# First input ahead of the settings, the feed-forward of the last batch but one behind the last scores, the last gelu from PSUM, and projections in the scores' ring of PSUM banks

## What is computed

```python
q = layer_norm(transpose(x + pos))      # b, 512, 256
kv = layer_norm(transpose(ctx + pos))
Q, K, V = split(q @ Wq), split(kv @ Wk), split(kv @ Wv)     # 16 heads of 16
y = softmax(Q @ K.T / 4) @ V @ Wo
r = y + q
h = layer_norm(r)
out = gelu(h @ W1 + b1) @ W2 + b2 + r   # W1 256x512, W2 512x256
return transpose(out)
```

## Time and profile before

| | |
|---|---|
| median of 3 runs | 3221.22 us |
| lowest, highest | 3213.65, 3223.86 us |
| the profiled execution | 3225.38 us |
| its span in the trace | 3223.6 us |
| mean granted TensorE clock | 0.939 |
| PE busy | 2833.4 us (88%) |
| DVE busy | 1797.5 us (56%) |
| ACT busy | 1350.6 us (42%) |
| POOL busy | 881.5 us (27%) |

### The profile page before, as it was taken

The page is one execution under the profiler, slowest core; times in us unless marked ns, Lnnn a source line. Parts: engine busy times, 40 slices in busy tenths (PEclk is TensorE's granted clock), DMA queues, the critical chain, the costliest instruction groups (busy, mean ns, idle before and its releaser), DMA issues. The chain is left out here.

```text
span 3223.6 us, 41533 instructions
## 1 busy us (share of the span) xinstructions
PE 2833.4 (88%) x14752; PEld 1332.4 (41%) x14752; DVE 1797.5 (56%) x4426; ACT 1350.6 (42%) x2376; POOL 881.5 (27%) x722
## 2 busy tenths in 40 slices
PE   4999999888999999989999999987868888888895
PEld 1222222234555555546556555643322333333332
DVE  3777777724344433312565565656777577667641
ACT  0566666652333333332434333422324444555462
POOL 1577777763344443310010001011111010100000
PEclk7999999998999999899999999998978999999997
DMA  4444444320002000112333323234233232323300
GB/s 101 94 106 101 108 102 103 96 88 26 27 28 84 28 28 22 69 51 72 68 65 63 65 65 75 50 70 91 73 90 86 58 85 51 87 65 68 75 26 21
DMA packets 182335, 219.94 MB, mean 68 GB/s; under 512 B 40840, under 2 KB 135664, under 8 KB 175984
## 3 DMA queue, kind: packets, MB, share of 16 engines
q1 hardware_dynamic: 170064, 189.74, 25.6%
q0 software_dynamic: 6016, 20.98, 1.9%
q10 hardware_dynamic: 6048, 6.56, 0.6%
HBM read 146.90 MB, written 51.64 MB: 62 GB/s over the span
## 5 line engine op out<-in xcount | busy, mean ns | idle before, releaser
L1485 DVE TENSOR_REDUCE l_M<-PS 128x1 f32<-128x512 f32 x512 | 334.5, 682 | 148.1 <-PE PS L963 145.2
L1264 DVE TENSOR_REDUCE l_M<-PS 128x1 f32<-128x512 f32 x512 | 332.0, 684 | 149.0 <-PE PS L704 148.1
L1203 ACT ACTIVATE l_P<-PS 128x512 f32<-128x512 f32 x512 | 286.7, 598 | 258.2 <-PE PS L973 240.5
L1568 POOL TENSOR_TENSOR l_S<-l_P 128x512 f32<-128x512 f32 x256 | 328.0, 1313 | 88.7 <-ACT l_P L1046 88.7
L1046 ACT ACTIVATE l_P<-PS 128x512 f32<-128x512 f32 x512 | 281.4, 598 | 111.4 <-PE PS L713 109.8
L963 PE MATMUL PS<-l_KS,l_QS 97*128 97x512 bf16 x512 | 206.3, 413 | 105.2 <-DVE l_M L1485 73.7
L1323 DVE TENSOR_REDUCE l1a_M<-PS 128x1 f32<-128x512 f32 x256 | 158.8, 682 | 246.4 <-PE PS L768 246.4
L1391 DVE CUSTOM_DVE_ANT_0 l_JK<-PS,l_MK 128x256 f32<-128x256 f32 x512 | 195.7, 419 | 136.2 <-PE PS L881 133.2
L704 PE MATMUL PS<-l_KS,l_QS 97*128 97x512 bf16 x512 | 204.2, 414 | 45.3 <-DVE l_M L1264 20.1
L846 PE MATMUL PS<-l_w_mlp_w,l_H 128*128 128x512 f32 x512 | 233.4, 602 | 5.9 <-ACT l1a_P L1099 5.0
L594 PE MATMUL PS<-l_YT,l_w_mlp_w 128*128 128x256 f32 x1024 | 233.3, 384 | 2.9 <-ACT l_YT L1124 2.6
(11 more groups left out here) (248 smaller groups left out, 4746.1 us busy)
## 6 DMA issues: line engine op xcount, KB each, us to landing
l_QS<-q_scratch SPq DMA_DIRECT2D x128, 128.0 KB, 5.7
q_scratch<-l_T SPq DMA_DIRECT2D x96, 128.0 KB
l_QS<-q_scratch SPq DMA_DIRECT2D x32, 384.0 KB, 4.9
k_scratch<-l_T SPq DMA_DIRECT2D x96, 128.0 KB
l_KS<-k_scratch SPq DMA_DIRECT2D x32, 384.0 KB
l_QS<-q_scratch SPq DMA_DIRECT2D x32, 256.0 KB, 5.5
l_KS<-k_scratch SPq DMA_DIRECT2D x32, 256.0 KB
l_RB<-l_recs SPq DMA_DIRECT2D x32, 256.0 KB
```

Source lines behind the costliest of these rows:

```text
L1203: e.activation(t.P[quad % 4][:, m, :], PS[:, COUNTS.bank[st], :], ACT.Exp, scale=0.25).then_inc(q.sem("act.exp", st), 1)
L1264: e.tensor_reduce(t.M[i % 2][:, qt, hd:hd + 1], PS[:, COUNTS.bank[st], :], AX.X, ALU.max).then_inc(q.sem("dve.smax", st), 1)
L1485: e.tensor_reduce(t.M[i % 2][:, qt, hd:hd + 1], PS[:, COUNTS.bank[st], :], AX.X, ALU.max).then_inc(q.sem("dve.smax", st), 1)
L1568: x = e.tensor_tensor(t.S[j % 2][:, m, :], t.P[2 * j % 4][:, m, :], t.P[(2 * j + 1) % 4][:, m, :], ALU.add)
```

## The change

It has five parts.

1. `0.start` on SP no longer holds the six `ones_rows`: they are a step of their own, `0.start1`, behind the first `0.load`. The first item's `stack` 0 moves from 0.36 to 0.52, behind the writes of both scratches.
2. In ring: `0.proj`, `0.turn`, `3.proj` and `3.turn` fill banks of ring C in place of ring A.
3. For batch 6 (the last but one) `f4` moves from 5.6 (and 0.08 each) to 6.36 (and 0.02 each), `f5` from 6.05 and 6.15 to 6.5 and 6.55: behind the last `sc` and `vals` of batch 7, ahead of the last `f1`.
4. For batch 7 the separate `gelu` is dropped: `f4` on ScalarE applies Gelu with the bias straight from PSUM to SBUF, and each product of `f5` waits for the quarter of `l_G` that it reads.
5. Each batch is stored in two halves, one behind each `f5`.

```diff
-        return [..., (0.36, k("stack", 0)), ...
+        return [..., (0.36 if (b, h) > (0, 0) else 0.52, k("stack", 0)), ...
-    return order + [(-9, ("0.start", 0, 0, 0)), ...]
+    return order + [(-9, ("0.start", 0, 0, 0)), (0.69, ("0.start1", 0, 0, 0)), ...]
-            out += [...] + [(5.6 + 0.08 * n, k("f4", n)) for n in range(4)]
-            out += [(6.05, k("f5", 0)), (6.15, k("f5", 1))]
+            out += [...] + [((6.36 + 0.02 * n) if b == B - 2 else (5.6 + 0.08 * n), k("f4", n)) for n in range(4)]
+            out += [(6.5, k("f5", 0)), (6.55, k("f5", 1))] if b == B - 2 else [(6.05, k("f5", 0)), (6.15, k("f5", 1))]
-        elif (kind, j) == ("3.f4", 3):
+        elif (kind, j) == ("3.f4", 3) and b < B - 1:
             cut = [(kind, b, h, j), ("3.gelu", b, h, 0)]
-FILLS = {"0.proj": ("A", "dve.rest"), ..., "0.turn": ("A", "act.turn"),
+FILLS = {"0.proj": ("C", "dve.rest"), ..., "0.turn": ("C", "act.turn"),
-         ... "3.proj": ("A", "dve.rest"), ... "3.turn": ("A", "act.turn"),
+         ... "3.proj": ("C", "dve.rest"), ... "3.turn": ("C", "act.turn"),
 (tensor3)
             elif kind == "3.f5":
                 q.wait_ge("w23", ("3.start2", 0, 0, 0))
-                q.wait_ge("act.gelu", step("3.gelu", i))
-                bank = q.bank_empty(st)
-                products(q, PS[:, bank, :], [(t.w2[:, o, j * 128:j * 128 + 128], t.G[:, o, :])
-                                             for o in range(4)]).then_inc(q.sem("pe.f5", st), 1)
+                if b < B - 1:
+                    q.wait_ge("act.gelu", step("3.gelu", i))
+                bank = q.bank_empty(st)
+                for o in range(4):
+                    if b == B - 1:
+                        q.wait_ge("act.f4", step("3.f4", i, o))
+                    x = e.matmul(PS[:, bank, :], t.w2[:, o, j * 128:j * 128 + 128], t.G[:, o, :], start=(o == 0), stop=(o == 3), ...)
+                x.then_inc(q.sem("pe.f5", st), 1)
 (scalar3)
-                e.activation(t.G[:, j, :], PS[:, COUNTS.bank[st], :], ACT.Identity, bias=col["b13"][:, j:j + 1]
-                             ).then_inc(q.sem("act.f4", st), 1)
+                e.activation(t.G[:, j, :], PS[:, COUNTS.bank[st], :], ACT.Gelu if b == B - 1 else ACT.Identity,
+                             bias=col["b13"][:, j:j + 1]).then_inc(q.sem("act.f4", st), 1)
 (sync0)
                 row(q, t.bv, "bv0")
-                q.wait_ge("pool.start", st)
+            elif kind == "0.start1":
+                q.wait_ge("pool.start", ("0.start", 0, 0, 0))
                 ones_rows(q, t.Q + t.K, 512)
 (sync3)
-            elif kind == "3.f5" and j == 1:
+            elif kind == "3.f5":
                 q.wait_ge("dve.f5", st)
-                e.dma_start(tokens(out[b]), t.RT[:, :, :]).then_inc(q.sem("store", st), 16)
+                e.dma_start(tokens(out[b])[:, j, :], t.RT[:, j, :]).then_inc(q.sem("store", st), 16)
```

More of the change, by code:

```diff
@@ L25, in a1 @@
         k = lambda n, j=0: ("0." + n, b, h, j)
-        return [(0.1125, k("proj", 0)), (0.1625, k("split", 0)), (0.3625, k("proj", 1)), (0.4125, k("split", 1)), (0.36, k("stack", 0)), (0.6, k("stack", 1)), (0.61, k("mrow")),
+        return [(0.1125, k("proj", 0)), (0.1625, k("split", 0)), (0.3625, k("proj", 1)), (0.4125, k("split", 1)), (0.36 if (b, h) > (0, 0) else 0.52, k("stack", 0)), (0.6, k("stack", 1)), (0.61, k("mrow")),
                 (0.6125, k("v", 0)), (0.8625, k("v", 1))]
@@ L52, in layer0_order @@
     order = [(2 * b + h + beat + at, st) for b, h in ITEMS for beat, part in enumerate((a0, a1, a2, c, p)) for at, st in part(b, h)]
-    return order + [(-9, ("0.start", 0, 0, 0)), (17.4, ("mark", 3, 0, 0)), (19.4, ("mark", 4, 0, 0))]
+    return order + [(-9, ("0.start", 0, 0, 0)), (0.69, ("0.start1", 0, 0, 0)), (17.4, ("mark", 3, 0, 0)), (19.4, ("mark", 4, 0, 0))]
 BEGIN1 = 18.35
@@ L149, in steps @@
             out += [(5.22 + 0.02 * n, k("onewton", n)) for n in range(3)] + [(5.3 + 0.03 * n, k("f2b", n)) for n in range(4)]
-            out += [(5.45, k("f3", 0)), (5.51, k("f3", 1))] + [(5.6 + 0.08 * n, k("f4", n)) for n in range(4)]
-            out += [(6.05, k("f5", 0)), (6.15, k("f5", 1))]
+            out += [(5.45, k("f3", 0)), (5.51, k("f3", 1))] + [((6.36 + 0.02 * n) if b == B - 2 else (5.6 + 0.08 * n), k("f4", n)) for n in range(4)]
+            out += [(6.5, k("f5", 0)), (6.55, k("f5", 1))] if b == B - 2 else [(6.05, k("f5", 0)), (6.15, k("f5", 1))]
         return out
@@ L273 @@
     "3.out1": [("put", 4, 1), ("me1", 1, 4)], "3.fetch": [("fetch", 2, 1)], "3.inv": [("rec", 2, 1)],
[1 row of a table removed]
[1 row of a table added]
 }
 JOINS = {("0.mrow", "ks"), ("0.sout1", "put"), ("1.sums1", "put"), ("2.out1", "put"), ("3.out1", "put")}
-FILLS = {"0.proj": ("A", "dve.rest"), "0.v": ("A", "dve.v"), "0.smax": ("A", "dve.smax"), "0.turn": ("A", "act.turn"),
+FILLS = {"0.proj": ("C", "dve.rest"), "0.v": ("A", "dve.v"), "0.smax": ("A", "dve.smax"), "0.turn": ("C", "act.turn"),
          "0.sc": ("C", "act.exp"),
@@ L699, in tensor0 @@
                 qt, hd = divmod(j, 8)
-                q.wait_ge("set", ("0.start", 0, 0, 0))
+                q.wait_ge("set", ("0.start1", 0, 0, 0))
                 q.wait_ge("qs", step("0.stack", i, 0))
@@ L1006, in tensor3 @@
                 q.wait_ge("w23", ("3.start2", 0, 0, 0))
-                q.wait_ge("act.gelu", step("3.gelu", i))
+                if b < B - 1:
+                    q.wait_ge("act.gelu", step("3.gelu", i))
                 bank = q.bank_empty(st)
-                products(q, PS[:, bank, :], [(t.w2[:, o, j * 128:j * 128 + 128], t.G[:, o, :])
-                                             for o in range(4)]).then_inc(q.sem("pe.f5", st), 1)
+                for o in range(4):
+                    if b == B - 1:
+                        q.wait_ge("act.f4", step("3.f4", i, o))
+                    x = e.matmul(PS[:, bank, :], t.w2[:, o, j * 128:j * 128 + 128], t.G[:, o, :], start=(o == 0), stop=(o == 3),
+                                 skip_group_check=True)
+                x.then_inc(q.sem("pe.f5", st), 1)
         def turn_act(q, st, y, i, MT, nh, w):
@@ L1213, in scalar3 @@
                 if k:
-                    q.wait_ge("store", step("3.f5", i - 2, 1))
+                    q.wait_ge("store", step("3.f5", i - 2, c))
                     x = e.activation(t.RT[:, c, :], PS[:, COUNTS.bank[st], :], ACT.Copy)
```

## The result

The changed kernel takes 3184.89 us (median of 4 runs, 3177.86 to 3190.24) against 3219.3 for the kernel before in the same comparison (4 runs, 3213.65 to 3223.86): a ratio of 0.9893, with a 95% interval of 0.9866 to 0.9919. That is 34.4 us less (by the interval 26 to 43). The forecast was 3188, in a range of 3170 to 3203, with 0.93 on faster. The profiled execution took 3190.24 us with a span of 3188.5.

The account below looks back on a forecast made before the run. TensorE and VectorE, neither full, were taken to wait on each other over PSUM banks, with serial start and end. Terms 12.5 + 6 + 0 + 8.7 + 6.0 + 0.3 = 33.5 off 3225.4, less 4.2 to the median: 3188 us, range 3170 to 3203.

Parts of the forecast that it names:

- The start: Up to layer 0's first scores: earlier input and reordered scratch transfers bring them 12.5 us sooner (9 to 14).
- the reordered round trip: Scratch transfers before the first scores: keys' writes directly follow queries', both stacks in flight together, scores at 31.1.
- Ring C in layer 3: Layer 3's projections: shorter TensorE stalls and VectorE holes at 23 waits for l_F, half counted, 6 us.
- More: Rival, 10%: in layer 3 the clock rises and all 27.9 us of l_F waits vanish; 3152 at its far end.
- Ring C in layer 0: Layer 0's projections and turns: 0 us, bounds -3 and +5, as waits for l_F are only 3.4.
- Batch 6's feed-forward: Serial end: last vals 19 us sooner once this work moves behind the last scores, net 8.7 us (5 to 11).
- Gelu from PSUM: Batch 7's feed-forward: f5 starts with the first quarters as f4 ends, second addition 6.0 us sooner.
- The drain: Gelu's table load at the end: no drain, by the profile; by the Trainium skill's rule 1.4 later, sum 3189.
- The halved stores: End of the kernel: half of the store goes out early, 0.3 us (0 to 1).
- Slower: Rival, 3%: projections in the scores' ring wait for a late ScalarE, stalling both engines at 64 projections; 3258 us.
- The start does nothing: Rival, 4%: first scores hang on something that does not move; 3200 us, with ring C's gain 3194.
- Less at both ends: Rival, 20%: shared DMA engines leave 8 of 12.5, layer 3's ring 0 of 6, the end 12 of 15; 3201 us.

Follow-up runs that it names:

- e13: Kernel before with only the first input moved ahead of the settings on SP, the stack in its old place: ratio 0.9985 (0.9967 to 1.0002).
- e9: Kernel before with only the first stack of queries moved behind the writes of both scratches: first scores 4.4 us sooner in one run, whose total says nothing.
- e2: Kernel before with only layer 0's projections and turns in ring C: 3219.94 us, ratio 0.9981 (0.9962 to 0.9999).
- e12: Kernel before with layer 0's projections and turns in ring C for all items but the first: 3214.51 us, ratio 0.9977 (0.9958 to 0.9996).
- e8: Changed kernel with the last spread ahead of batch 6's first store on SP: 3183.92 us, ratio to the kernel before 0.9867 (0.9845 to 0.9889).
- e7: Kernel before with only batch 7's gelu from PSUM and the halved stores: 3219.63 us, ratio 0.9994 (0.9977 to 1.001).
- e1: Kernel before with only the start changed (input ahead of settings, both scratch writes ahead of the first stack): 3216.61 us, ratio 0.9972 (0.9951 to 0.9992).
- n1: Changed kernel with batch 6's f5 moved behind Wo of batch 7: 3174.56 us, ratio to the kernel before 0.9852 (0.9832 to 0.9872).

## Why the prediction was right, step by step

The sign, the size (33.5 forecast, 34.4 measured, 26 to 43 by the interval) and the chain at the end were right. Two terms of the sum were wrong in opposite directions, by -1.3 and about +6 us, so that the two totals agree within 1 us is partly luck.

- **The start: 12.5 forecast, 11.2 measured.** The input was right (6.4; to the first product 6.8 in the changed kernel and 6.6 in e13, to the first scores 6.9 in e13). Its landing of 7.3 us from 1.66 to 8.95 is 0.7 over the earlier trace rows. By the Trainium skill, page "DMA: Bandwidth & Descriptors", section "Issuing engines are not separate DMA queues", queues of two engines share the DMA engines. That rule holds here: `WvT` landed 10.3 us behind its issue in place of 6.5, and the first product of keys waited 1.16 for `l_C`. But the cost fell mainly on transfers that were needed later, so its price for this term was nearer to 0.7 than to the 3.4 of the far bound. The step that failed is the reordered round trip: 6.1 forecast, 4.4 measured (e9). The sentence "I take 31.1, nearer the first" took off 0.6 for two stacks in flight; they cost 1.3 in e9 and 2.1 in the changed kernel. The other traces with the old start reach the first scores 0.6 to 0.9 us sooner than the kernel before, so the 11.2 could as well be read as 10.3 to 10.7.
- **Ring C in layer 3: 6 forecast, 6.8 measured** (interval 0.6 to 12.6), with the waits moved as described: `l_F` from 27.9 to 12.1 ("under 20"), and 7.1 to 10.3 us taken up by the maxima. The mechanism is shown, the size is not: in the trace of the changed kernel layer 3 itself is 0.3 us shorter. "More" (all of 27.9, and a higher clock in layer 3) fell: 12.1 of the wait stayed, and the clock of the middle is 0.92 where it was 0.91.
- **Ring C in layer 0: 0 forecast, about 6 measured** (e2 and e12). The step that failed reads "Layer 0: 3.4 us is all there is, TensorE is the engine waited for". It priced the ring by one row of waits. The projection's own wait for a bank, 5.5 us in 11 places, stood under another line (594) in the same list; and even both together are not what was gained, since in e2 TensorE is idle in layer 0 for as long as before (64.7 us). Its busy time fell from 599.8 (590.1 to 599.5 in the other kernels with ring A) to 584.9 us, at a higher clock; 5.1 of the fall lie between the first scores and the first turn. The prediction has such a term of the clock in its rival "more", but for layer 3 alone.
- **Batch 6's feed-forward: 8.7 forecast, about 8.9 measured** (14.8 from the last `turn` to the end in all, less the 5.9 of parts 4 and 5). The last `vals` came 15.1 behind the one that counts, Wo 24.3 behind it, `spread` directly behind the store. The 2 us that I put on this store are confirmed by e8, which found 2 more in the clock behind it.
- **Gelu from PSUM: 6.0 forecast, 5.8 measured** (35.81 to 30.00; 5.9 in e7). Behind the transposes it gave 6.7, and 0.9 went back to Wo's slower clock (0.53 in the changed kernel; 0.72 from 3179 to 3185 before), which the forecast had not seen. The reason "gelu's table is now there from batch 6" isn't needed, as e7 shows.
- **The drain.** The table load ended at 3135.87 and gelu began at 3135.89, and in e7 the Gelu follows its load as closely. The Trainium skill's 1380 ns (page "ScalarE: Activation LUTs", section "What ACT_TABLE_LOAD costs") don't appear in the changed kernel either.
- **The halved stores: 0.3 forecast, 0.06 measured.** The time from the last addition to the end was 8.51 and is 8.45.
- **The rivals.** "Slower" needed ScalarE to be late for ring C: the `sc` of layer 3 wait 26.8 us for exps, against 29.7 before. "The start does nothing" fell with e1. "Less at both ends" was right in its crowding (11.2 in place of 12.5) and wrong elsewhere.

The four parts alone give 9.0 + 6.1 + 6.8 + 15.8 = 37.7 us by their ratios, all together 34.4; the intervals of the parts (6 to 7 us to either side each) are too wide to tell that from a plain sum.

## What to carry to other kernels

When a step is moved from one ring of buffers to another, collect every wait that its place in the ring causes, its own for the buffer as well as its successors' for its release; they stand under different lines. Then compare the engine's idle and busy time over the same work, between the same two steps, and not in a window of fixed times: here the waits only moved, and the gain was in the busy time. When work must be placed near a serial end, look for the gap of the chain itself (here a layer norm on VectorE with TensorE idle for 5.8 us) before placing it ahead of the chain, and keep its store out of a queue that the chain uses: in place, that was worth another 9.7 us over the changed kernel. Where a single trace drifts by more than the effect, read each part in place at its anchor and let many runs decide the total.

## What was not expected of the hardware

A short gap left the clock as it was, and longer ones didn't, but the time doesn't follow their length. The same 16 products of Wo took 3.72 us behind 1.44 us of idle time (clock 1.00), 6.46 behind 3.37 (0.53), and 6.74 behind 5.99 (0.50). Behind 13.21 us they took 5.19 in the kernel before (clock 0.72 from 3179 to 3185), and 6.25 behind 13.25 in e7 (0.59). In n1 `f5`, which follows Wo without a gap, ran at a clock of 1.00 again. A gap shortened by 2 us was thus worth 4 in e8.
